# Routing tables and slot search of a 64-expert layer moved ahead of the first expert, and the shared FFN's products moved to VectorE

## What is computed

```python
# 1 causal linear attention, 16 heads of 8:  out = (q . cumsum(k v)) / max(q . cumsum(k), eps), q, k = elu(.) + 1
# 2 mixture of experts: 64 experts, 8 per token, capacity 160 rows per expert, FFN 384
shared_out = _swiglu(x, shared_w1, shared_w2)        # (x @ w1.T) split in halves, x1 * silu(x2) @ w2.T
gates = softmax(x @ wg.T);  w_topk, idx_topk = top_k(gates, 8);  w_topk /= w_topk.sum()
rank = arange(A) - starts[se]                        # place of a (token, expert) pair in its expert
buf = zeros((64, 160, H)).at[se, rank].set(x[st])    # dispatch
out = (x1 * silu(x2)) @ expert_w2                    # of h = buf @ expert_w1, for each expert
combined = zeros((T, H)).at[st].add(out[se, rank] * sw);  return shared_out + combined
# 3 four encoder layers (linear attention without mask, FFN 512 with relu)
# 4 a router that sends 75% of each sequence through gelu(x @ w_block)
```

## Time and profile before

| | us |
|---|---|
| median of 3 runs | 752.38 (752.27 to 756.96) |
| profiled execution, device time | 748.92 |
| its span in the profile | 747.1 |
| TensorE busy in the span | 583.6 (78%) |
| VectorE busy | 454.8 (61%) |
| GpSimd busy | 359.2 (48%) |
| ScalarE busy | 235.2 (31%) |

### The profile page before, as it was taken

One profiled execution on the slowest core, in us unless ns is written; L12 is line 12 of the kernel. 1 busy time (PEld: TensorE's weight loads), 2 busy tenths in 40 slices (PEclk: granted clock), 3 DMA queues, 4 the chain that ended last, 5 costly groups with the idle time before them and its releaser, 6 DMA issues.

```text
span 747.1 us, 11154 instructions
## 1 busy us (share of the span) xinstructions
PE 583.6 (78%) x3747; PEld 485.0 (65%) x3747; DVE 454.8 (61%) x1401; ACT 235.2 (31%) x447; POOL 359.2 (48%) x357
## 2 busy tenths in 40 slices
PE   6998877967958697979797032579999999999861
PEld 5767644666958586878796022458777877877641
DVE  4677655616646333323343268887778778777995
ACT  3133245212212122212232010134344344443564
POOL 4655122775465555666456449742243233234342
PEclk9998998879989899889899555689999999999995
DMA  8950000125555566657573660000000000000001
GB/s 306 415 218 22 22 8 21 43 64 180 155 183 170 178 202 202 212 187 236 194 226 95 254 267 1 0 1 12 4 29 11 4 28 11 4 28 1 1 2 57
DMA packets 29565, 79.43 MB, mean 106 GB/s; under 512 B 7104, under 2 KB 12096, under 8 KB 29264
## 3 DMA queue, kind: packets, MB, share of 16 engines
q1 hardware_dynamic: 23088, 65.69, 25.6%
q0 software_dynamic: 6432, 13.16, 6.0%
HBM read 62.60 MB, written 16.25 MB: 106 GB/s over the span
## 4 chain that ended last, share of the span: by engine, by line
PE 58%; DVE 15%; issue 8%; another core or an unknown queue 7%; ACT 4%; POOL 4%; DMA 2%; SPq 0%; DVEq 0%; POOLq 0%; ACTq 0%
PE bank L768 12%; PE bank L904 6%; PE bank L892 6%; PE bank L778 5%; PE bank L525 4%; PE bank L834 3%; PE bank L852 2%; PE bank L815 2%; PE bank L829 2%; DVE stats L253 2%; PE bank L843 2%; PE bank L870 2%; POOL rstd L268 2%; PE bank L557 1%
## 5 line engine op out<-in xcount | busy, mean ns | idle before, releaser
L268 POOL TENSOR_TENSOR rstd<-veps,minus_half 128x4 f32<-128x4 f32 x52 | 53.9, 1037 | 208.0 <-DVE veps L261 205.7
L768 PE MATMUL bank<-hidden,ring 128*128 128x160 f32 x768 | 126.7, 316 | 3.7 <-issue 2.6
L1318 POOL DMA_INDIRECT returned_rows<-x1t,scatter_all x80 | 81.0, 1013 | 81.7 <-DVE x1t L1692 62.5
L768 PEld LDWEIGHTS bank<-hidden,ring 128*128 128x128 f32 x768 | 116.5, 205 | 5.2 <-issue 3.7
L1119 ACT ACTIVATE hidden<-bank 128x480 f32<-128x480 f32 x64 | 36.9, 576 | 185.7 <-PE bank L768 136.3
L778 PE MATMUL bank<-hidden,ring 128*128 128x160 f32 x384 | 68.4, 315 | 19.7 <-DVE hidden L1681 16.4
L778 PEld LDWEIGHTS bank<-hidden,ring 128*128 128x128 f32 x384 | 58.3, 199 | 24.0 <-DVE hidden L1681 19.1
L1669 DVE COPY hidden<-bank 128x384 f32<-128x384 f32 (+1 forms) x32 | 23.3, 732 | 78.1 <-PE bank L768 55.1
L1170 ACT ACTIVATE arena<-bank,layer_cols 128x512 f32<-128x512 f32 x64 | 44.0, 687 | 62.6 <-PE bank L892 62.6
L815 PE MATMUL bank<-consts,arena 128*128 128x128 f32 x192 | 28.4, 284 | 44.1 <-DVE arena L292 44.1
L904 PE MATMUL bank<-ring,arena 128*128 128x128 f32 x512 | 59.9, 275 | 1.4 <-issue 1.4
(11 more groups left out here) (210 smaller groups left out, 1195.0 us busy)
## 6 DMA issues: line engine op xcount, KB each, us to landing
ring<-in_ew SPq DMA_DIRECT2D x64, 576.0 KB
returned_rows<-zeros SPq DMA_DIRECT2D x16, 512.0 KB, 14.9
arena<-returned_rows SPq DMA_DIRECT2D x6, 512.0 KB, 11.8
hidden<-returned_rows SPq DMA_DIRECT2D x4, 512.0 KB, 5.0
ring<-returned_rows SPq DMA_DIRECT2D x4, 512.0 KB, 7.9
ring<-in_l1w SPq DMA_DIRECT2D x8, 256.0 KB, 2.7
returned_rows<-x1t,scatter_all POOLq DMA_INDIRECT x80
shared<-in_xr SPq DMA_DIRECT2D x1, 1024.0 KB, 7.9
```

The source lines that it names most:

```text
L268: pool.tensor_tensor(rstd[:, s, :], veps[:, s, :], minus_half[:], ALU.pow).then_inc(sem(f"rstd{which}_ready"), 1)
L768: mm = pe.matmul(bank[2 * (n % 2) + part][:, CAP * f:CAP * f + CAP], ring[:, n % RING, P * (FB * part + f):P * (FB * part + f) + P], E["xt ...
L1318: pool.indirect_dma_start(returned_dram[:, :], bass.IndirectOffsetOnAxis(ap=scatter_all[:, Q, b:b + 1], axis=0), E["back"][:, Q % BACK, b, ...
```

## The change

- *Shared FFN.* ScalarE no longer copies the plain half; VectorE multiplies it straight from its bank with the Silu result (`shared_product`). Groups 0 and 1 (SOON = 2) are done in front of the experts, with hidden pieces in six buffers of their own and rows in bank 7. Groups 2 and 3 are done behind the last expert: x1 is transposed again (`turn_late`), six pieces (`late_hidden`), rows in banks 4 and 5, which VectorE adds to x1 from the bank (`add_base`, all four groups; GpSimd's additions go).
- *Order in front.* Pieces (0, 0) and (0, 1) stand behind the last output projection, the others behind the last logits and ranks. ScalarE's `scale_gates` of group 2 moves behind the last norm. The high part of the last group is converted by VectorE. Four low tables are built for the 12 known tiles while the last group is routed, and finished for the last 4 tiles later.
- *Tables.* High tables are built for 2 quads and then for the other 14 in one go: three operations of 640 and three of 4,480 elements. `b_code` and `token16` are stored spread out for it (ScalarE makes them in the loop's second turn).
- *Searches.* Five calls (FOUND) of 1, 1, 2, 2 and 2 quad pairs, all of them, with their index steps, before the first expert. Nothing of it is left in the expert loop. Experts wait for `shared_ready` of 2 groups.

The core of the diff:

```diff
-            return ((0, 2), (3, 4), (5, 6))[0 if m == 0 else 1 + m % 2]
+            return ((0, 2), (5, 6), (3, 4), (5, 6), (0, 2), (3, 4))[m]
+        FOUND = ((0,), (1,), (2, 3), (4, 5), (6, 7))
...
-                if g == GROUPS - 1:
-                    shared_hidden(0, 0)
                 sum_products(g, 7)
                 sum_heads(g, 3)
             ranks(GROUPS - 2)
             attention_out(GROUPS - 1, 1)
+            shared_hidden(0, 0)
             shared_hidden(0, 1)
+            turn_x1(GROUPS - 1)
+            route_logits(GROUPS - 1)
             shared_hidden(0, 2)
-            turn_x1(GROUPS - 1)
+            ranks(GROUPS - 1)
             shared_hidden(1, 0)
-            route_logits(GROUPS - 1)
             shared_hidden(1, 1)
...
+            find_slots(0)
             shared_rows(0)
             shared_hidden(1, 2)
+            find_slots(1)
+            shared_rows(1)
+            for call in range(2, len(FOUND)):
+                find_slots(call)
...
-            pe.wait_ge(sem("shared_ready"), GROUPS)
+            pe.wait_ge(sem("shared_ready"), SOON)
...
-                if j == 1 and Q + 2 < NEG // 2:
-                    pe.wait_ge(sem("xt_read"), 2 * (Q + 1))
-                    if Q >= 2:
-                        pe.wait_ge(sem("back_read"), 2 * (Q - 1))
-                    find_slots(Q + 2, bank[6])
...
+            for g in range(SOON, GROUPS):
+                turn_late(g)
+            for f in range(FB):
+                late_hidden(SOON, f)
+            late_hidden(SOON + 1, 0)
+            late_rows(SOON)
+            late_hidden(SOON + 1, 1)
+            late_hidden(SOON + 1, 2)
+            late_rows(SOON + 1)
...
-                act.activation(hidden[:, FB + f, :], bank[up][:], ACT.Silu)
-                act.activation(hidden[:, f, :], bank[plain][:], ACT.Copy).then_inc(sem("hidden_read"), 1)
+                act.activation(hidden[:, m, :], bank[hidden_banks(m)[0]][:], ACT.Silu).then_inc(sem("hidden_read"), 1)
...
             pool.wait_ge(sem("rows_out"), 16 * 2 * GROUPS)
-            for b in range(RB):
-                gather_block(0, b)
-            shared_products(2)
-            for b in range(RB):
-                gather_block(1, b)
-            shared_products(3)
-            for Q in range(2, AHEAD):
+            for Q in range(AHEAD):
                 for b in range(RB):
                     gather_block(Q, b)
...
-                elif Q + AHEAD < NEG + GROUPS:
-                    g = Q + AHEAD - NEG
-                    pool.wait_ge(sem("shared_ready"), GROUPS)
-                    pool.tensor_tensor(tiles(shared, g), tiles(shared, g), tiles(x1, g), ALU.add).then_inc(
-                        sem("base_ready"), 1)
...
+            def high_tables(first, last):
+                es, n = slice(EG * first, EG * last), EG * (last - first)
+                wide = [P, RB, TILES, n]
+                hit = b_out[:, 0:RB, :, es]
+                ch.after(ch.did(v.tensor_tensor(hit, b_in[:, :, es].unsqueeze(1).to_broadcast(wide),
+                                                codes_b[:, :, es].unsqueeze(2).to_broadcast(wide), ALU.is_equal)))
+                ch.after(ch.did(v.tensor_tensor(b_out[:, RB:2 * RB, :, es], hit,
+                                                place[:, :, es].unsqueeze(1).to_broadcast(wide), ALU.mult)))
+                ch.after(ch.did(v.tensor_tensor(hit, hit, token[:, :, es].unsqueeze(1).to_broadcast(wide), ALU.mult)))
...
-            EARLY = 6
-            for Q in range(EARLY):
-                low_table(Q)
-                high_table(Q)
-                if Q in (1, 3):
-                    indices(Q // 2, bank[1])
+            shared_product(0)
+            shared_product(1)
+            v.wait_ge(sem("codes_ready"), 2)
+            v.wait_ge(sem("bi_ready"), GROUPS - 2)
+            for Q in range(4):
+                low_table(Q, 0, KNOWN)
+            best_of(GROUPS - 1)
+            masks_of(GROUPS - 1)
+            places_of(GROUPS - 1)
+            split_ranks(GROUPS - 1)
+            v.wait_ge(sem("b_index"), GROUPS)
+            v.tensor_copy(group_of(bi16, GROUPS - 1), group_of(logits_i, GROUPS - 1)).then_inc(sem("bi_ready"), 1)
+            invert_sums(GROUPS - 1)
+            v.wait_ge(sem("bi_ready"), GROUPS)
+            high_tables(0, 2)
+            for Q in (0, 1):
+                low_table(Q, KNOWN)
+            indices(0)
+            for m in (2, 3, 4):
+                shared_product(m)
+            high_tables(2, NEG)
+            for Q in (2, 3):
+                low_table(Q, KNOWN)
+            low_table(4)
+            indices(1)
+            shared_product(5)
+            for call in (2, 3, 4):
+                for Q in range(4 * call - 4, 4 * call):
+                    if Q > 4:
+                        low_table(Q)
+                if call > 2:
+                    indices(call - 1)
+            indices(4)
...
+            for g in range(SOON):
+                add_base(g)
+            for m in range(FB * SOON, FB * SOON + 4):
+                late_product(m)
+            add_base(SOON)
+            for m in range(FB * SOON + 4, FB * GROUPS):
+                late_product(m)
+            add_base(SOON + 1)
```

More of the change, by code:

```diff
@@ L215, in program @@
         B.update(carve([("relu", (2, FFB, GROUP), F32)], at_relu))
+        SOON = 2
+        late = [B["kp"][:, m] for m in range(GROUPS)] + [B["eq"][:, m] for m in range(2)]
+        late = [(a if len(a.shape) == 2 else a.rearrange("p i d -> p (i d)")) for a in late]
         layer_cols = sb("layer_cols", [LAYERS, LP])
@@ L383, in hidden_banks, with call_of, slot_bank @@
         def hidden_banks(m):
-            return ((0, 2), (3, 4), (5, 6))[0 if m == 0 else 1 + m % 2]
+            return ((0, 2), (5, 6), (3, 4), (5, 6), (0, 2), (3, 4))[m]
+        FOUND = ((0,), (1,), (2, 3), (4, 5), (6, 7))
+        def call_of(Q):
+            return [Q // 2 in qs for qs in FOUND].index(True)
+        def slot_bank(call):
+            return bank[(1, 6)[call % 2]]
         def group_of(buf, g):
@@ L1132, in _ @@
                     keep_result(n - LAG)
+            for g in range(SOON, GROUPS):
+                act.wait_ge(sem("turned_x1"), GROUPS + g - SOON + 1)
+                act.activation(B["ht"][:, g], bank[4 + g % 2][:], ACT.Copy).then_inc(sem("x1t_ready"), 1)
+            for m in range(FB * SOON, FB * GROUPS):
+                act.wait_ge(sem("hidden_mm"), m + 1)
+                act.activation(late[m - FB * SOON], bank[2 * (m % 2) + 1][:], ACT.Silu).then_inc(sem("hidden_read"), 1)
             def norm1_columns(n, g, l):
@@ L1642, in indices @@
-            def indices(q, to):
-                qs = slice(2 * q, 2 * q + 2)
-                v.wait_ge(sem("slots_mm"), q + 1)
-                v.tensor_tensor(picked[:], to[:, 0:4 * RB * EG].rearrange("p (u b e) -> p u b e", u=2, e=EG),
-                                own.unsqueeze(1).unsqueeze(1).to_broadcast([P, 2, 2 * RB, EG]), ALU.mult).then_inc(
-                    sem("slots_read"), 1)
-                v.wait_ge(sem("slots_read"), q + 1)
-                ch.after(ch.did(v.tensor_reduce(slots[:, qs].rearrange("p g t b -> p g (t b)"), picked[:], AX.X, ALU.add)))
+            KNOWN = GT * (GROUPS - 1)
@@ new lines, in indices @@
+            def indices(call):
+                n = 2 * len(FOUND[call])
+                qs = slice(2 * FOUND[call][0], 2 * FOUND[call][0] + n)
+                v.wait_ge(sem("slots_mm"), call + 1)
+                v.tensor_tensor(picked[:, 0:n], slot_bank(call)[:, 0:2 * RB * EG * n].rearrange(
+                    "p (u b e) -> p u b e", u=n, e=EG), own.unsqueeze(1).unsqueeze(1).to_broadcast([P, n, 2 * RB, EG]),
+                    ALU.mult).then_inc(sem("slots_read"), 1)
+                v.wait_ge(sem("slots_read"), call + 1)
+                ch.after(ch.did(v.tensor_reduce(slots[:, qs].rearrange("p g t b -> p g (t b)"), picked[:, 0:n], AX.X,
+                                                ALU.add)))
```

195 lines of the change are left out of this document (95 added, 100 removed).

## The result

The kernel after the change takes 733.59 us (median of 4, 730.58 to 733.83) against 752.33 (median of 4, 750.42 to 756.96) beside it: a ratio of 0.972, interval 0.967 to 0.977. The forecast was 728.4. The gain came out at 18.7 us by the medians and 15.2 by the profiled executions (748.92 to 733.74), where the sum said 24.0.

What follows compares the result with a forecast made beforehand. The prediction saw a chain of waits with no engine full, and a gather lock of 15.65 us per quad among the experts. Its terms, -9.4 - 7.3 - 8.1 + 0.8 = -24.0, gave 728.4 us; 8-in-10 range 706 to 744.

Steps and rivals of the forecast that it cites:

- Steps a to c: Before the first expert: shared FFN moved out, high bits converted by VectorE, all tables and searches in front; first expert -9.4 us.
- step a: Last attention group: shared FFN moved out of it, so best-of-8 comes at 111.2 instead of 116.09, -4.9 us.
- Step d, first half: First expert to first scatter: no search, table or index step left, late results put at 1.9 us; -7.3 us.
- the hold: Expert loop: TensorE's results are seen late while gathers are issued, giving 15.65 us per quad; predicted to stay.
- Step d, second half: Expert loop, quad 0 to 4: 70.72 us become four turns of 15.65, 62.6 us; -8.1 us.
- Step e: Behind the experts: two shared groups take 20.0 us, mostly covered by the wait for returned rows; +0.8 us.
- the prediction's own sign of being wrong: Behind the experts: wrong if VectorE's late products, not the returned rows, release the first sum; no size given.
- Lock gone: Rival, expert loop: the hold disappears and ten issues, 12.5 us, bound ten quads; 31 us more gain, 697; chance 0.15.
- GpSimd starved by the tables: Rival, early gathers: twenty each wait 1.2 to 2.5 us for tables, delaying the first scatter; +6, 734; chance 0.08.
- Late groups on the low clock: Rival, behind the experts: TensorE's clock falls and 16.2 us of late work become 31; +15, 743; chance 0.10.
- contended pace: Rival, before the experts: tables beside gathers run slowly, VectorE's stage grows some 35 us; 763, slower; chance 0.05.
- The stalls return: Rival, early quads: late results stall them as before, so only the front's gain remains; 743; chance 0.07.

Runs made afterwards that it cites:

- four quads ahead: Against the kernel after, gathers run four quads ahead instead of six, so those of quads 4 and 5 stand behind scatters of quads 0 and 1; 732.6 us.
- the order with two scatters last: Against the kernel after, GpSimd issues three scatters, five gathers, two scatters per quad; 674.55 us on chip B, 675.4 on chip C (0.971 of the kernel before).
- the mixed order: Against the kernel after, GpSimd issues three scatters, two gathers, two scatters, three gathers per quad instead of five scatters, five gathers; 726.2 us on chip A.

## Why the prediction was right and wrong

All in us, from the timelines (chip A stands for the profiles of the measurement); "best" is the best-of-8 of the last group:

| stretch | predicted | chip A: before to after | chip C: before to after |
|---|---|---|---|
| start to best | -4.9 | -4.6 (116.09 to 111.53) | +0.3 (111.56 to 111.82) |
| best to first expert | -4.5 | -4.4 | -5.0 |
| first expert to first scatter | -7.3 | **-0.5** (32.7 to 32.2) | -3.8 (26.7 to 22.9) |
| first scatter to quad 10's | -8.1 | -6.7 (164.7 to 158.1) | -4.8 (133.0 to 128.2) |
| quad 10's to quad 15's scatter | 0 | -0.3 | **-4.4** |
| quad 15's scatter to first sum | +0.8 | +0.8 | +1.1 |
| the rest | 0 | +0.4 | -1.3 |
| sum | -24.0 | -15.3 | -18.0 |

*Steps a to c* came out within 0.4 us together, step a partly by luck. Inside them, tables started 1.4 us late, at 117.4, because VectorE waited 1.11 us for ranks behind a shared piece at the lower clock, and the rest of the stage took 1 us less than reckoned. What a was worth differs from one trace of the kernel before to the other. It reached the last output projection at 102.94 in the first and at 100.08 on chip C, 2.9 us that no edit explains, and this is part of the -4.6. The sum also misread a row: the 1.71 us at 112.37 are one half of the last pair ahead of the logits, and the whole pair took 2.74 (111.34 to 114.08) in the chain, its second half at the lower clock. On chip C the same pair took 1.02 us a half, and the eight logits matmuls 1.00:

```profile
110.04 1.00 PE L608 MATMUL bank<-sw,x1t 128*128 128x64 f32 x8
```

In the kernel after the same eight take 1.97, on chip A as on C, behind a wait of 2.29 us:

```profile
107.76 0.66 PE L610 MATMUL bank<-consts,x 128*128 128x128 f32 x4 [2.29 <-ACT x L286]
109.10 1.97 PE L622 MATMUL bank<-sw,x1t 128*128 128x64 f32 x8 [0.69 <-ACT x1t L1067]
```

The granted clock of 100 to 118 us is 0.81 in both traces of the kernel after, 0.91 in the first profile of the kernel before, and 1.00 in it on chip C. I had taken the two removed pieces as pure gain. From the transposes (L596, now L610) to best-of-8 it went from 5.40 us to 3.77 in the measurement, 1.6 for the 2.74 taken out, and from 3.73 to 3.94 on chip C, nothing for 1.7: the copy of the transposes (0.6 us), which the pair had covered, now stands in the open, and the logits matmuls run at the lower clock. The wait alone doesn't explain the clock, since the kernel before waits 3.16 us at this place in both its traces, loses the clock in one and keeps it in the other; the cause was not tried.

*Step d, first half, is the term that was mis-sized*: "The gathers of quads 4 and 5 still fall into it, so results may come late there: between 0 and the 10.6 us of before (32.7 - 22.1). I take 1.9, near the lower end, since the stalls of before sat at index waits". It measured 8.7 over the 23.5 us of an unhindered start (22.1 + 1.4), and 3.5, 3.6 and 6.9 in the three other traces of chip A with these gathers. The reason given for the low end was wrong: the kernel after has no index wait here and takes 32.2 us, hardly less than the 32.7 of before. If chip C is taken as the pace without the hold, the hold was 6.0 us of it before (32.7 - 26.7) and 9.3 after (32.2 - 22.9), while what the change took out of the loop is the 3.8 us by which chip C got faster: quad 4's gathers now follow quad 3's at once and fall on experts 1 and 2. The run with four quads ahead shows it from the other side, at 24.15, and the kernel after on chip C, with the same gathers, at 22.9. The value was taken at the wrong end of the stated bounds. (The upper bound itself counts the last 1.4 us twice; over 23.5 the stall of before was 9.2.)

*Step d, second half* forecast 1.4 too much gain: the loop took 15.8, not 15.65 (15.64 in the three other kernels with gathers on chip A). What made it up, issues, hold and 1.4 us back to a scatter, agrees with the runs without gathers (10.88) and on chip C (12.82: ten issues are 12.8 and not 12.5). "That it holds while gathers are issued I can" read from the trace is right, and right for one kind of chip alone.

*Step e* came out at the predicted +0.8, by luck. The sum had VectorE late. The work itself took what the sum said, 19.7 us against 20.0 (from the first late transpose at 389.50 to the end of the last addition at 409.15), but it waits 0.28 us for the rows, and the 0.8 are in the reload: its last load for the first sum took 7.0 us to land (402.78 to 409.79) where it took 6.2 in the kernel before (419.24 to 425.44). In the four other traces of chip A the first sum follows VectorE's own work without a wait for the rows, the prediction's own sign of being wrong, and starts 10.5 us behind the last scatter, no later than the 10.7 here. The last sentence of the step, "the four GpSimd additions between scatters leave a queue with room: 0", is right on chip A (-0.3). On chip C the queue has no room, the scatters of the last quads stand 7.6 us apart with an addition of 1.3 between them and 6.4 without, and moving them off is worth 4.4 us.

*The rivals.* "Lock gone" named 697 for a kernel that would shed the hold by itself; neither did, but another chip can, and then it is 676. Of the 21 us between them 18 are in one stretch that the rival left as it was, quad 10's to quad 15's scatter (50.6 us in the kernel before, 32.5 on chip C). "GpSimd starved by the tables" is the one whose time, 734, came out, and half of its mechanism did: the 15 gathers beside tables took 24.9 us of issue (means 2.00, 1.63 and 1.35 in quads 0, 1 and 2; the longest 2.86) where the first 15 of the kernel before took 16.3, and the last of quads 0 to 3 ended at 158.1 instead of 148. Each of the three issues beside a big table ends the same time behind it:

```profile
126.09 2.49 DVE L1659 TENSOR_TENSOR arena<-arena,place 128x4480 f16<-128x4480 f16 x1
```
```profile
127.19 2.22 POOL L1340 DMA_INDIRECT arena<-dispatch_rows,gather_all  x1 [0.30 <-issue]
```

This table ends at 128.58 and the gather issue at 129.41, 0.83 us later; the first big table (123.58 + 2.48) and the issue of 2.86 us (124.03) end 0.83 us apart too, the third pair 0.82. So these issues last until the table is through, which agrees with a lock; no run took the tables away to show it. The Trainium skill says that a VectorE operation with two SBUF inputs and a GpSimd operation that reads SBUF exclude each other for a whole instruction (SBUF — State Buffer, "SBUF: two separate sides"). The tables have two such inputs and a gather reads its indices from SBUF, so the ends agree with that rule. The Trainium skill also reports a probe in which operations of this kind (tensor_tensor) did not stall a DMA (SBUF — State Buffer, "Who interferes with whom"); the issues here grew to 2.86 us beside them, and the measurement decides. But the starving alone costs nothing: on chip C the same gathers are as long (mean of the first 20 in both: 1.48) and the first scatter comes at 175.23. Together with the hold it may cost: it puts quad 4's gathers at 158.43 to 164.4, beside experts 1 and 2, instead of some us earlier. How much of the 8.7 us that is wasn't tried. On chip C the same effect shows in the kernel before inside the loop: its issues beside tables reach 1.90 us, and the first three turns take 14.2 to 14.9 us instead of 12.8, which is where its 4.8 us are; whether by the tables alone wasn't tried apart. "Late groups on the low clock" and "contended pace" fell: late pieces ran at the upper level (1.02 us) and tables at their medians. "The stalls return" was right up to the first scatter (32.2 us against 32.7) and wrong behind it, where the loop ran at one pace.

*Open.* What on chip A keeps TensorE's results from being taken up while gathers are under way is not known. The ends of matmuls are modelled in these traces, so a result that is seen late and a matmul that in truth ends late look the same; the pauses inside groups of twelve matmuls say that TensorE itself is disturbed. VectorE and ScalarE take up its results at one moment (both at 166.76). Whether the order with two scatters last covers the hold was not tried where there is one. On chip C no version beat the kernel after beyond the uncertainty.

## What to carry to other kernels

Repeat the kernel before, with a profile, beside every experiment, and compare its own traces with one another before a step's number is believed: here a 57 us difference between chips would have been read as an effect of the edit. Where a step moves work so that a burst of transfers falls on a new neighbour, take its cost from the rows in which that burst and such a neighbour meet, and not from the wait which happened to stand beside it. Behind a piece taken out of TensorE's stream, look at the granted clock of the pieces that follow: part of the gain can go there.

## What was not expected of the hardware

- The same program, 755 us on chip A (752 in the measurement), 695 and 697 on two others. A gather issue (0.95 us) and an undisturbed group of twelve matmuls (1.80, its end modelled) are of the same length on both kinds; on chip A groups break up beside gathers, and their results are taken up as much as 7.9 us late (expert 1 of the kernel after, 158.86 to 166.76).
- On chip A the hold hangs on gathers (DRAM to SBUF, issued by GpSimd) and not on scatters of the same queue or on the weight loads: 10.88 us a quad without the first, 15.6 without the last.
- Three traces with the same code up to there, of the pace of chip A, reached the first scatter 27.0, 27.1 and 32.2 us behind the first expert, and of the 7.5 us between the kernel after (733.7) and the one with the mixed order (726.2) 5.3 were there at the first scatter.
- A gather issue beside a VectorE table lasts until 0.82 to 0.83 us behind the table's end, in three pairs one behind the other.
